# A block of two mixture-of-experts layers around a recurrent mixer on one core: weights sent with the rows, adding gathers, other group sizes

## The reference, cut to what matters

```python
x = x + 0.5 * ffn(layernorm(x))        # x: 8 sequences x 512 tokens x 128 channels, fp32
x = x + attn(layernorm(x))
x = x + 0.5 * ffn(layernorm(x))

def ffn(x):                            # 8 experts, the best 2 for each token
    probs = softmax(x @ gate_w)
    expert_weights, expert_indices = top_k(probs, 2)
    expert_weights /= expert_weights.sum(-1, keepdims=True)
    for i in range(8):
        wi = where(expert_indices == i, expert_weights, 0).sum(-1)
        h = silu(x @ w1[i]) * (x @ w3[i])          # 128 -> 512
        out += (h @ w2[i]) * wi[..., None]         # 512 -> 128

def attn(x):                           # x mixed with its shifted self, per channel
    k, v, r = xk @ Wk.T, xv @ Wv.T, sigmoid(xr @ Wr.T)
    return (r * wkv(k, v, time_decay, time_first)) @ Wo.T   # wkv: a scan over the 512 tokens
```

## Time and profile before

| | |
|---|---|
| median of 3 runs | 689.54 us (688.97 to 691.28) |
| the profiled execution | 690.3 us |
| its span | 688.5 us |
| PE busy | 518.2 us, 75% |
| DVE busy | 430.6 us, 63% |
| ACT busy | 334.9 us, 49% |
| GpSimd busy | 264.7 us, 38% |

### The profile page before, as it was taken

The page is one execution under the profiler, slowest core; times in us unless marked ns, Lnnn a source line. Parts: engine busy times, 40 slices in busy tenths (PEclk is TensorE's granted clock), DMA queues, the critical chain, the costliest instruction groups (busy, mean ns, idle before and its releaser), DMA issues.

```text
span 688.5 us, 16328 instructions
## 1 busy us (share of the span) xinstructions
PE 518.2 (75%) x5128; PEld 462.3 (67%) x5128; DVE 430.6 (63%) x1314; ACT 334.9 (49%) x717; POOL 264.7 (38%) x267
## 2 busy tenths in 40 slices
PE   0300789899989889987962359989879989999920
PEld 0200679889878689765961139977769989999920
DVE  4490488675647599426987959786678683425402
ACT  0640546545584744777442435654856544444400
POOL 1067007556634320134101742415451547246244
PEclk9999999999999999999995579999998999999975
DMA  8991113223322222112100122221222333334222
GB/s 278 345 304 50 49 41 98 86 85 95 89 69 73 55 58 63 50 45 50 53 12 7 51 76 62 79 59 48 69 61 68 86 97 113 89 97 109 79 57 65
DMA packets 87564, 58.88 MB, mean 86 GB/s; under 512 B 9792, under 2 KB 81216, under 8 KB 87488
## 3 DMA queue, kind: packets, MB, share of 16 engines
q1 hardware_dynamic: 79296, 41.05, 20.3%
q0 software_dynamic: 8192, 16.79, 8.6%
HBM read 28.65 MB, written 29.16 MB: 84 GB/s over the span
## 4 chain that ended last, share of the span: by engine, by line
PE 26%; DVE 11%; POOL 6%; issue 5%; ACT 4%; DMA 2%; POOLq 0%; DVEq 0%; ACTq 0%
PE py L966 9%; PE pa L953 7%; PE pb L953 7%; POOL rows_in L528 4%; DVE h L844 2%; POOL yg L542 2%; DVE xres L854 1%; PE pT L941 1%; ACT L590 1%; ACT xn L608 1%; DMA rows_in<-parts,slot 1%; ACT sil L590 1%; DVE shared L915 1%; DMA rin<-rows_in 1%; DVE stats L687 0%
## 5 line engine op out<-in xcount | busy, mean ns | idle before, releaser
L844 DVE TENSOR_TENSOR h<-sil,pb 128x512 f32<-128x512 f32 x177 | 120.8, 687 | 177.7 <-ACT sil L590 130.7
L528 POOL DMA_INDIRECT rows_in<-parts,slot x128 | 136.9, 1070 | 210.4 <-DVE slot L789 81.7
L542 POOL DMA_INDIRECT yg<-rows_out,slot x128 | 125.9, 984 | 205.7 <-DVE h L844 158.4
L966 PE MATMUL py<-ffn_w,h 128*128 x1416 | 195.3, 282 | 7.6 <-ACT yrow L584 7.5
L966 PEld LDWEIGHTS py<-ffn_w,h 128*128 128x128 f32 x1416 | 175.1, 195 | 12.2 <-issue 8.2
L953 PE MATMUL pa<-rT,ffn_w 128*128 128x128 f16 (+1 forms) x1440 | 151.6, 248 | 21.1 <-ACT rT L579 10.9
L953 PE MATMUL pb<-rT,ffn_w 128*128 128x128 f16 (+1 forms) x1440 | 153.7, 247 | 0.0
L953 PEld LDWEIGHTS pa<-rT,ffn_w 128*128 x1440 | 114.5, 100 | 38.5 <-issue 26.9
L953 PEld LDWEIGHTS pb<-rT,ffn_w 128*128 x1440 | 114.7, 99 | 9.6
L590 ACT ACTIVATE sil<-pa 128x512 f32<-128x512 f32 x177 | 104.9, 593 | 22.5 <-PE pa L953 21.9
L584 ACT ACTIVATE yrow<-py 128x128 f32<-128x128 f32 x177 | 49.0, 277 | 114.3 <-PE py L966 113.1
(11 more groups left out here) (126 smaller groups left out, 454.1 us busy)
## 6 DMA issues: line engine op xcount, KB each, us to landing
rows_out<-yrow SPq DMA_DIRECT2D x177, 64.0 KB
rin<-rows_in SPq DMA_DIRECT2D x57, 128.0 KB
shared<-in_w SPq DMA_DIRECT2D x16, 256.0 KB, 6.0
rin<-rows_in SPq DMA_DIRECT2D x63, 64.0 KB
rows_in<-zrow SPq DMA_DIRECT2D x2, 1984.0 KB, 10.6
rows_in<-zrow SPq DMA_DIRECT2D x2, 1472.0 KB, 11.5
xres<-in_x SPq DMA_DIRECT2D x4, 512.0 KB, 7.4
ffn_w<-in_w SPq DMA_DIRECT2D x8, 256.0 KB, 6.5
```

Source lines behind the costliest of these rows:

```text
L528: pool.indirect_dma_start(rows_in[g][:], bass.IndirectOffsetOnAxis(ap=slot[:, c, at:at + 1], axis=0), parts[:, at, :], None).then_inc(s_sc ...
L542: pool.indirect_dma_start(yg[:, b, c, j, :], None, rows_out[SET[run]][0:STEPS[run] * T, :], bass.IndirectOffsetOnAxis(ap=slot[:, c, at:at ...
L844: dve.tensor_tensor(h[:, t % RING, :], sil[:, t % 2, :], pb[t % 2][:], ALU.mult).then_inc(s_h, 1)
L966: mm = pe.matmul(py[:], h[:, (FIRST_STEP[q] + c // per) % RING, at:at + T], w, start=(c == 0), stop=(c == FC - 1))
```

## The change

- **Runs.** `FIRST = (1, 2, 3, 2)`. Runs now begin at tiles 0, 15, 38, 69, 92, 123, 154. Run 0 is unit 0, run 1 units 1 and 2, run 2 units 3 to 5, run 3 units 6 and 7.
- **Weights in the rows.** A row in `rows_in` has 129 fp32 words (516 bytes) instead of 512 bytes: the last is the token's routing weight, by which ACT scales `yrow` (`scale=`). The row has the first choice's weight first; before the second choice is scattered, GpSimd waits for the unit's first scatters and copies the second weight in.
- **Adding gathers.** A gather adds to `xres` in the transfer (`compute_op=ALU.add`). The second waits for the first of the same block. `combine` is gone.
- **Order of transfers**: first choices of all units of a run, then second choices (gathers: by unit).
- **Ranks.** The counts of a run are summed by PE in PSUM (`count` has 2 matmuls for each block), so `place` and `place2` have fewer operations. `rsqrt` has 11 operations instead of 13.
- **Start.** The splits stand in the plan between the steps of the first route; the fills stand behind w1 and w3 on SP's queue; semaphores for the small loads are apart. `rin` has 7 places instead of 3, still loaded 3 ahead.

```diff
-FIRST = (2, 2, 2, 2)
+FIRST = (1, 2, 3, 2)
...
+    plan += [(EARLY, "split", 0, 0), (EARLY, "rsqrt", 0, 0)]
     plan += [(EARLY, step, 0, b) for b in early for step in ("norm", "hi")]
+    plan += [(EARLY, "split", 0, 1)]
+    plan += [(EARLY, "lo", 0, b) for b in early]
...
-        many = [(u, j, c) for u in ([b] if name == "gather" else range(UNITS[run])) for j in range(JU)
-                for c in range(TOPK)]
+        many = [(u, j, c) for c in range(TOPK) for u in ([b] if name == "gather" else range(UNITS[run]))
+                for j in range(JU)]
...
+            load_x(0)
+            sp.dma_start(gate_w[:], gate).then_inc(s_gate, 16)
+            sp.dma_start(vecs[:], channel_vecs).then_inc(s_vecs, 16)
+            stage(0)
+            stage(1)
+            load_x(1)
+            for e in range(2, E):
+                stage(e)
+            sp.wait_ge(s_zrow, 1)
+            fill(0, 0, STEPS[0] * T, s_fill)
+            sp.dma_start(att_raw[:], att_w).then_inc(s_attw, 16)
...
+                if (j, c) == (0, 1):
+
+                    pool.wait_ge(s_sc0[b], 16 * JU * len([r for r in range(run + 1) if UNITS[r] > b]))
+                    pool.tensor_copy(weight_col[:, js], wts[:, 1, js]).then_inc(s_second, 1)
+                    pool.wait_ge(s_second, sum(UNITS[:run]) + b + 1)
                 pool.indirect_dma_start(
                     rows_in[g][:], bass.IndirectOffsetOnAxis(ap=slot[:, c, at:at + 1], axis=0),
-                    parts[:, at, :], None).then_inc(s_scat[g], 16)
+                    rows_sb[:, at, :], None).then_inc(s_scat[g] if c else s_sc0[b], 16)
...
+                if c:
+                    pool.wait_ge(s_first[b][j], 16 * additions(run, b))
                 pool.indirect_dma_start(
-                    yg[:, b, c, j, :], None, rows_out[SET[run]][0:STEPS[run] * T, :],
-                    bass.IndirectOffsetOnAxis(ap=slot[:, c, at:at + 1], axis=0)).then_inc(s_gat[b], 16)
+                    xres[:, at, :], None, rows_out[SET[run]][0:STEPS[run] * T, :],
+                    bass.IndirectOffsetOnAxis(ap=slot[:, c, at:at + 1], axis=0), compute_op=ALU.add
+                    ).then_inc(s_both[b] if c else s_first[b][j], 16)
...
-                act.activation(yrow[:, t % YSLOTS, :], py[:], ACT.Copy).then_inc(s_yrow, 1)
+                q, block, _ = TILE_OF[t]
+                act.activation(yrow[:, t % YSLOTS, :], py[:], ACT.Copy,
+                               scale=rin[:, q % SLOTS, block, D:RW]).then_inc(s_yrow, 1)
...
-            def combine(run, b):
...
+                    if name == "mstats":
+                        dve.wait_ge(s_both[b], 16 * JU * additions(run, b))
```

More of the change, by code:

```diff
@@ L75 @@
        ("att", 11), ("out", 13), ("add", 13)]
-CHOOSE = [("pick", 0), ("pick2", 0), ("count", 2), ("place", 2), ("place2", 2), ("scatter", 2), ("tiles", 3),
-          ("weights", 3)]
-FINISH = [("combine", 0), ("write", 3)]
+CHOOSE = [("pick", 0), ("pick2", 0), ("count", 2), ("place", 2), ("weights", 2), ("place2", 2), ("scatter", 2),
+          ("tiles", 3)]
+FINISH = [("write", 0)]
 MIX_DONE = [step for step, _ in MIX].index("att") + 1
@@ L201, in make_plan @@
                                                   if c.steps is CHOOSE and c.run < run)
-                        or any(step in COST[eng] and load[eng] >= ROOM[eng] for eng in COST)):
+                        or run != 1 and any(step in COST[eng] and load[eng] >= ROOM[eng] for eng in COST)):
                     break
@@ L213, in make_plan @@
                     ask(clock + 1, START[run] - 3, "scatter", run, 0)
-    last = [(TILES, step, RUNS - 1, b) for step in ("gather", "combine", "write") for b in range(UNITS[-1])]
+    last = [(TILES, step, RUNS - 1, b) for step in ("gather", "write") for b in range(UNITS[-1])]
     return plan + last, transfers
@@ L374, in macaron_kernel @@
         s_fill = [sem(f"rows_zeroed{g}") for g in range(SETS)]
+        s_rest = [sem(f"more_rows_zeroed{g}") for g in range(SETS)]
         s_const = sem("const_made")
@@ L394, in macaron_kernel @@
         s_eid = sem("tile_experts_made")
+        s_wts = sem("weights_made")
+        s_sc0 = [sem(f"first_scattered{b}") for b in range(UG)]
+        s_second = sem("second_weights_set")
         s_scat = [sem(f"scattered{g}") for g in range(SETS)]
@@ L427, in units, with additions @@
             return u, slice(u * JU, (u + 1) * JU)
+        def additions(run, b):
+            return [p[2] for p in PLAN if p[1] == "gather" and p[3] == b].index(run) + 1
         def xn_slot(name, run, b):
@@ L461, in _ @@
             for g in range(1, R1):
-                fill(g)
+                fill(g, 0, STEPS[g] * T, s_fill)
                 if g > 1:
                     load_x(g)
+            for g in range(SETS):
+                if ROWS[g] > STEPS[g] * T:
+                    fill(g, STEPS[g] * T, ROWS[g], s_rest)
             def load(q):
@@ L486, in step @@
                     u, js = units(run, b)
-                    sp.wait_ge(s_comb, count(("combine",), ("combine", run, b)))
+                    sp.wait_ge(s_both[b], 16 * JU * additions(run, b))
                     sp.dma_start(ov[:, js, :], xres[:, js, :]).then_inc(s_out, 16)
-            for q in range(SLOTS):
+            for q in range(AHEAD):
                 load(q)
             for t in range(TILES + SKEW + 1):
-                if t < TILES and TILE_OF[t][1] == 0 and TILE_OF[t][0] + SLOTS < QSTART[RUNS]:
-                    load(TILE_OF[t][0] + SLOTS)
+                if t < TILES and TILE_OF[t][1] == 0 and TILE_OF[t][0] + AHEAD < QSTART[RUNS]:
+                    load(TILE_OF[t][0] + AHEAD)
                 if t > SKEW:
@@ L863, in step @@
                 k, v, r = kk[:, u % 2, :], vv[:, u % 2, :], tr[:, u % 2, :]
-                if name == "combine":
-                    combine(run, b)
+                if name == "split":
+                    split(b)
                 if name in ("stats", "mstats"):
```

263 lines of the change are left out of this document (132 added, 131 removed).

## The result

The changed kernel takes **714.77 us** (median of 4 runs, 711.91 to 716.81), the kernel before 690.29 beside it: a ratio of 1.035 (95% interval 1.032 to 1.039). The forecast was 670 and faster, with a range of 653 to 691. It was wrong in sign and the time lies outside the range. Every ratio here leaves out the runs that lie over 1.5% above the fastest of their kernel, while a median given beside it is that of all runs.

The account below looks back on a forecast made before the run. PE sets the pace where tiles run; the rest is waiting at the start, before runs 4 and 5, and in the tail. Terms summed to -19.8 us from 690.3, hence 670.5, stated as 670, range 653 to 691.

Parts of the forecast that it names:

- I take 31.5, since 4 bytes more is nearest to one packet: Start: 31.5 ns for each 516-byte fill packet, putting h(0) at 61.8 us instead of 76.4, -14.6.
- the same formula: Start: h(0) is 50.9 us, plus 0.81 for each ns a packet takes over 26.9, plus 7.2.
- The upper end: Start: a 516-byte row priced as two packets, 54 ns, with h(0) at 80.0 us.
- rows of 516 bytes cost two packets: Rival at the start: h(0) at 80.0 us, 18.2 later than in the sum, 688 in all; chance 0.12.
- the start's sum: Start: routing chain to h(0) at 53.8 us, then SyncE's queue dry at 54.6 and h(0) at 61.8.
- An adding gather costs GpSimd twice: Rival at the gathers: an adding gather takes twice a plain one's slot, 703 us, slower; chance 0.10.
- 16x and 24x - 17.6: Cost of x us more per adding gather: 16x in the tail, 24x - 17.6 before run 4; break-even x = 0.93.
- what DVE loses lies beside it: 0: Tiles 123 to 176: PE is 98% busy, so relieving DVE changes nothing, 0 us.
- Tail, "-2.3": Tail: the adds of 2.31 us and nothing else go, -2.3 us (-3 to +2).
- I give back a quarter, -5: Tiles 15 to 89: a quarter of PE's 20.9 us idle is won back, -5 us (0 to -11).
- the forecast's 3.7 more: Tile 37: two scatters gated on h(35) bring h(37) 9.9 us after it, +3.7 us.
- Runs 1, 4 and 5: Waits for scatters: h(14) +10.3 us, gap before run 4 -26.1, gap before run 5 +11.2.

Follow-up runs that it names:

- late: Changed kernel with the fills of later tables cut in pieces and issued behind the first loads of `rin`: 689.43 us, 0.998 of the kernel before.
- all3: Changed kernel with 576-byte rows, later fills in pieces behind the first loads, and plain gathers with adds on VectorE: 665.34 us, 0.963 of the kernel before.
- plain: Changed kernel with plain gathers into a buffer of their own and the adds back on VectorE: 697.76 us, 1.012 of the kernel before.
- before1232: Kernel before with only the first groups changed to 1, 2, 3 and 2, on a slower chip: 761.01 us, 0.997 of the kernel before.
- pad576: Changed kernel with rows padded from 516 to 576 bytes: 698.03 us, 1.011 of the kernel before.
- rate2: Changed kernel with all3's edits, run 1's ranks before tile 0, and 2.0 planned transfers a tile instead of 1.6; slower chip: 755.26 us, 0.992 of the kernel before.
- all3b: Repeat of all3 on a slower chip: 726.01 us, 0.969 of the kernel before.
- rate2b: Repeat of rate2 on a slower chip: 747.37 us, 0.992 of the kernel before.
- rate2c: Repeat of rate2 on a faster chip: 660.79 us, 0.956 of the kernel before.

## Why the prediction failed

- **The step that failed first: "I take 31.5, since 4 bytes more is nearest to one packet".** That SyncE's queue binds the start, its bytes and, nearly, the overlap (1.15, measured 1.18) were right: with 57.7 ns in place of 31.5 the same formula gives 83.0, and 83.5 was measured (in part by luck, as said under its table: the queue ended 2.4 us later, and 5.3 us stood behind it and not 7.2). The upper end, two packets or 54 ns, was about what such a row took over the whole start (54.6), and less than in the stretch of fills alone (57.7). The rival "rows of 516 bytes cost two packets", at 0.12, came nearest in its h(0), 80.0, but each row was one packet. I ordered the two ends by length, and the cause is where the row begins and ends: 544 bytes cost 35 ns, 516 from a multiple of 32 bytes 43, 516 from any 58 to 70 (means of the stretch from 36 to 48 us).
- **The rule on the row's beginning.** The rule of the Trainium skill that the forecast cites (DMA: Bandwidth & Descriptors, "How a descriptor splits into AXI transactions"), extra beats for a row that starts off a 256-byte boundary, gave an estimate of 33 ns for 516 bytes, and the trace does not agree: 57.7. Rows of 544 bytes start off that boundary too and took 35.0. For them the same rule gives some 34 ns, again an estimate, so it prices those rows and misses what 516 bytes add. A line elsewhere in the Trainium skill (Collectives: The Full Stack, "Rules for kernel authors") fits better, though it is said of the buffers of collectives: they are to be aligned to 32 bytes, which "Prevents HW read-modify-write". That the transfers here read and merge is not shown by any run; that 32 bytes is enough is.
- **The fills' place in the queue.** I saw that SyncE's queue would bind the start and took it as given. late shows that it was free to change: 25 us.
- **The start's weight copy** stood in the start's sum at nothing, and in the later runs at 0.3 us, its operation. It is a wait for a landing, 9.73 us here. It was hidden behind the queue in the changed kernel, and is on the path once that is dry: all3's h(0) beats late's by 6.6 us, about as much as that wait is shorter (6.5).
- **"An adding gather costs GpSimd twice"** was a rival with a break-even of 0.93 us more each, and the sum itself charged nothing; it was 0.60. By my formula, 16x and 24x - 17.6, that is 9.6 us. plain shows 17. The tail's part holds (8.1 measured, with a landing of 3.4 us). Missing is what is queued behind the wait for a gather. The planner gives a gather the time that it gave before, two steps, and what waits for it stands earlier in the list. At tile 84 DVE stands 4.6 us in front of `stats`, an `h` stands behind it, and PE waits 3.5 us for that: 3.1 us of the 9.4 between the two kernels in that stretch. The rest is spread over tiles (1.8 at tile 15, 1.3 at tile 87, less elsewhere) and was not traced.
- **Tiles 123 to 176, "what DVE loses lies beside it: 0"**: the engine that was missed is SyncE. Its wait in front of the write of a unit, with the load of `rin` behind it, accounts for the 4.9 us: tile 171 takes 5.1 us more than with plain gathers.
- **Tail, "-2.3"**: with plain gathers it is still 35.2 us and not 31.5. These 3.7 us are no part of the adding gather's price, and why they are there stays open.
- **Tiles 15 to 89, "I give back a quarter, -5"**: with plain gathers the stretch is 234.0 us, 3.2 less than before; with adding ones 6.2 more. Tiles 36 and 37 took 9.3 us instead of 5.7, the forecast's 3.7 more, so the relief itself was some 8 us, within the stated 0 to 11, and the adding gathers ate about all of it.
- **Runs 1, 4 and 5**: right, by the stated counts. In the gap before run 4 the 20 scatters took 29.9 us and not 26.9, which is the whole 3 us. One reason given there is not supported: I credited the lighter chains too, and before1232 has the gap at 35 us without them.

In sum: the row, moved on a queue that binds the start, missed by 21.7 us, and of the 23 in the later stages the adding gather accounts for 17, by the medians of plain. With both undone and the fills late the kernel takes 665.

## What to carry to other kernels

When a word is added to a row that is moved in bulk, pad the row to a multiple of 32 bytes before judging the idea, and take the price of a transfer as engine time over packets in a stretch where the engines are full, not as the typical packet. A transfer that adds takes the work from VectorE and puts it on the queue that issues, once per use, and on every in-order engine that waits for it: where GpSimd ends the run, as it does here, it costs more than it saves. Put work that nobody needs yet (fills of later tables) behind the first load that somebody waits for.

## What the hardware showed unexpectedly

- In the changed kernel the 516-byte packets from 36 to 48 us had a median of 44 ns and a mean of 58; one in ten took over 101 ns, the longest 655. Of the 576-byte ones (median and mean 35) one in ten took over 40. They slow others too: 512-byte packets of other loads took 35.1 ns on average over the start of the changed kernel and 30.7 in pad576. The scatters' packets took 436 ns in that stretch (4,128 bytes, median) against 230 in pad576 (4,608 bytes), but they write rows of 516 bytes themselves.
- Two of the chips were slower than the others: the kernel before took 760.7 and 752.6 us against 690.3 to 691.0 (9 to 10%), all3 9% more, rate2 13 to 14% more. The mean granted clock was alike in all3 (0.928 and 0.930), but in h(122) to h(176) it was 0.97 in all3b against 1.00 in all3, and the kernel before had 0.94 on the faster chips and 0.92 on the slower. That stretch took 161.1 us against 135.3, while start, gaps and tail were within 1 us. In it PE was busy 143.9 us and idle 17.2 in all3b, against 132.6 and 2.7 in all3; DVE's `h` took 687 ns on both. Loads of instructions don't explain it: their 16 KB packets took 1181 ns in all3b against 1064 in all3 (median), but 1054 in rate2 on a slower chip (rate2b) against 1125 on a faster one (rate2c). The cause stays open.
